# Masking the two large units of turned scores on TensorE instead of VectorE, with new orders on every engine and a setup that is split up among the first turns

## The reference

```
def _L0_attn_ref(X, ...):                     # one head, no mask
    A = softmax(Q K^T * scale);  return A V
def _L0_ffn_ref(x, w_gate, w_up, w_down):     # FP4 quantised inputs and weights
    h = silu(fp4_linear(x, w_gate)) * fp4_linear(x, w_up)
    return fp4_linear(h, w_down)
def _L1_attn_ref(inputs, qkv_kernel, qkv_bias):   # 16 heads of 8
    qk = jnp.einsum('bhse,bhte->bhst', q, k) * scale
    mask = jnp.triu(jnp.full((s, s), -jnp.inf, dtype=jnp.float32), k=1)
    attn = jax.nn.softmax(qk + mask, axis=-1)
def _L1_ffn_ref(x, gate_w, w1, w2, w3):       # 4 usable experts of 704, top 2 per token
    h = silu(x w1) * (x w3);  y = h w2;  out = sum of the two chosen
mod = (_silu(c) @ wmod)                       # 6 rows of 128 per sample and layer
x = x + ga * attn(layernorm(x) * (1 + ca) + sa)
x = x + gb * ffn(layernorm(x) * (1 + cb) + sb)   # this pair of lines twice
```

## Time and profile before

| | |
|---|---|
| profiled execution, span | 1905.3 us |
| the same execution's time | 1907.06 us |
| median of three runs | 1906.21 us |
| TensorE (PE) busy | 1699.7 us, 89% of the span |
| VectorE (DVE) busy | 1678.0 us, 88% |
| ScalarE (ACT) busy | 716.5 us, 38% |
| GpSimd (POOL) busy | 68.9 us, 4% |

### The profile page before, as it was taken

One profiled execution on the slowest core, in us unless ns is written; L12 is line 12 of the kernel. 1 busy time (PEld: TensorE's weight loads), 2 busy tenths in 40 slices (PEclk: granted clock), 3 DMA queues, 4 the chain that ended last, 5 costly groups with the idle time before them and its releaser, 6 DMA issues.

```text
span 1905.3 us, 37018 instructions
## 1 busy us (share of the span) xinstructions
PE 1699.7 (89%) x12297; PEld 1317.1 (69%) x12297; DVE 1678.0 (88%) x3791; ACT 716.5 (38%) x1447; POOL 68.9 (4%) x78
## 2 busy tenths in 40 slices
PE   2347799999999999999999999999999999999998
PEld 1234567776776767677686767777676777768787
DVE  5578799989899998989989998999989899997775
ACT  0122435262533426253432526243352525334332
POOL 0000000000000000000000000000000000000000
PEclk7686899999999999999999999999999999999999
DMA  4020302003030301203030110303021030303000
GB/s 142 25 76 28 109 5 89 28 20 98 5 107 10 104 14 27 86 15 97 10 105 13 50 63 18 99 5 106 12 63 51 18 99 6 100 10 91 12 13 8
DMA packets 130106, 97.25 MB, mean 51 GB/s; under 512 B 28000, under 2 KB 124512, under 8 KB 125824
## 3 DMA queue, kind: packets, MB, share of 16 engines
q1 hardware_dynamic: 121536, 91.74, 16.4%
q10 hardware_dynamic: 8448, 4.20, 0.7%
HBM read 56.48 MB, written 29.98 MB: 45 GB/s over the span
## 4 chain that ended last, share of the span: by engine, by line
PE 47%; DVE 37%; issue 9%; ACT 4%; SPq 1%; DVEq 1%; DMA 1%; POOL 0%; ACTq 0%; POOLq 0%
DVE mneg L1099 9%; PE y_ps L1476 9%; PE bank L1469 5%; PE bank L1471 5%; PE bank L1470 5%; DVE h L1196 4%; PE bank L1220 4%; DVE tt L1188 3%; PE bank L1436 3%; ACT arena L770 2%; DVE xh L967 2%; PE bank L1343 2%; DVE arena L1107 2%; PE bank L1373 2%; PE bank L1420 2%
## 5 line engine op out<-in xcount | busy, mean ns | idle before, releaser
L813 ACT ACTIVATE tt<-bank 128x512 f32<-128x512 f32 x352 | 212.4, 603 | 665.8 <-PE bank L1471 523.9
L1476 PEld LDWEIGHTS y_ps<-wd,h 128*128 128x128 f32 (+1 forms) x3072 | 379.1, 192 | 70.7 <-issue 19.1
L1476 PE MATMUL y_ps<-wd,h 128*128 128x128 f32 (+1 forms) x3072 | 415.4, 282 | 14.1 <-DVE h L1196 14.1
L1196 DVE TENSOR_TENSOR h<-tt,bank 128x512 f32<-128x512 f32 x352 | 236.0, 682 | 23.6 <-PE bank L1471 7.1
L1188 DVE SCALAR_TENSOR_TENSOR tt<-tt,bank 128x512 f32<-128x512 f32 x352 | 237.2, 682 | 21.4 <-ACT tt L813 14.7
L1099 DVE TENSOR_REDUCE mneg<-bank 128x2 f32<-128x512 f32 (+1 forms) x384 | 236.0, 680 | 3.9 <-issue 2.4
L770 ACT ACTIVATE arena<-bank 128x512 f32<-128x512 f32 x384 | 196.5, 612 | 34.8 <-PE bank L1417 20.7
L1469 PE MATMUL bank<-h_hi,wg_hi 128*128 128x512 f32 x352 | 164.2, 466 | 10.3 <-DVE h_lo L1163 3.8
L1469 PE MATMUL bank<-h_hi,wu_hi 128*128 128x512 f32 x352 | 163.1, 463 | 8.4 <-DVE mneg L1099 8.3
L1107 DVE TENSOR_TENSOR arena<-arena,keep_k 128x1024 f32<-128x1024 f32 (+1 forms) x96 | 149.0, 1577 | 20.4 <-ACT arena L770 18.8
L1471 PE MATMUL bank<-h_lo,wg_hi 128*128 128x512 f32 x352 | 140.5, 399 | 0.0
(11 more groups left out here) (183 smaller groups left out, 2647.0 us busy)
## 6 DMA issues: line engine op xcount, KB each, us to landing
q_stack<-q_rows SPq DMA_DIRECT2D x16, 1024.0 KB, 4.8
k_stack<-k_rows SPq DMA_DIRECT2D x16, 1024.0 KB, 8.0
q_rows<-qk_halves SPq DMA_DIRECT2D x48, 256.0 KB, 2.8
k_rows<-qk_halves SPq DMA_DIRECT2D x48, 256.0 KB, 2.9
rows<-mod_rows SPq DMA_DIRECT2D x48, 128.0 KB, 3.0
rows<-mod_rows SPq DMA_DIRECT2D x16, 384.0 KB, 3.5
x_in<-in_L_attn_X SPq DMA_DIRECT2D x16, 256.0 KB, 2.8
vals<-arena SPq DMA_DIRECT2D x128, 32.0 KB, 5.2
```

The source lines that it names most:

```text
L813: send(a(tt[:, ch % 2, :], ps.bank(f"eg{ch}")[:], ACT.Tanh, scale=0.5), tanh_ready)
L1196: frees(v.tensor_tensor(h32[:, ch % 3], tt[:, ch % 2, :], ps.bank(f"eu{ch}")[:], ALU.mult), f"eu{ch}")
L1476: ins = mm(y_ps[:, P * t:P * (t + 1)], h32[rows_, ch % 3, P * t:P * (t + 1)], wd[rows_, ch, :], start=first and t == 0, stop=last_ and t = ...
```

## The change

Four things are changed together.

1. *Masks.* `cover` is done for the four E units only (`covered` counts four instead of six). For L0 and L1, TensorE's `rows` first writes a mask to each of the four banks by `masked` with `mask_q` as the weights and `ident_b` as the moving side (a 128x512 bf16 matmul), and adds the sixteen products to it. `weigh` now waits for `covered` of its E unit and for ScalarE's last exponential of its L unit.
2. *Orders.* `USES` and the lists of SyncE, ScalarE, VectorE and TensorE are new. The point at which a turn begins has been moved as well: `maxima(5)`, `turn_max` and `stack_max` stood early in a turn with lead 1 and now stand at its end with lead 2.
3. *Setup loads.* The 31 loads of FP4 and expert weights are issued by ScalarE after its copy of the turned conditions. SyncE issues 15 small loads, the rows of ones and at once the first pair's `x_in`. The wait for the conditions counts four loads instead of all 15. The conditions lie in `mixed` instead of `x_in`, and the staging areas elsewhere in `arena`.
4. *Setup work.* The eight clamps become three wider ones. The two upper halves are copied by ScalarE. The rest is hung behind named steps of the first pair (`follow`): the quantisation of the first two weights behind `norm1`, the two lower halves behind `value0`, the third weight behind `quantise_x(2)` on VectorE; the turning of each weight on TensorE and its copy on ScalarE behind `scores0(1)`, `out0`, `probs0(1)` and `turn2`.

```diff
-SMALL = 15
+SMALL = 11
-USES = [(1, "SB30", "D", 6), (1, "SB31", "D", 5), ...
+USES = [(0, "eu6", "D", 3), (3, "T1", "A", 4), ...
 def sp_order(do):
-    do(1, "stack_v"), do(0, "load4"), do(1, "stack_max"), do(1, "load3"), do(1, "turn_att"), do(3, "load2"), do(4, "load1")
-    do(2, "store_q"), do(2, "store_k"), do(2, "stack")
+    do(1, "stack_v"), do(1, "load3"), do(0, "load4"), do(1, "turn_att"), do(3, "load2"), do(4, "load1"), do(2, "store_q")
+    do(2, "store_k"), do(2, "stack"), do(2, "stack_max")
...
-        covered = signal("covered", len(TURNED))
+        covered = signal("covered", len(EARLY))
...
-        def turns(eng, order, mine):
+        def turns(eng, order, mine, follow={}):
...
-                        mine[name](Turn(reg, plus + lead), *which)
+                        it = Turn(reg, plus + lead)
+                        mine[name](it, *which)
+                        if first_pair(it) and (name, *which) in follow:
+                            follow[(name, *which)]()
...
         def _(act):
-            act.wait_ge(s_ld, 16 * SMALL)
-            a(res[0:NB, 0:2, :], x_in[0:NB, 0:2, :], ACT.Tanh, scale=0.5).then_inc(s_act0, 1)
+            act.wait_ge(s_cond, 16 * 4)
+            a(res[0:NB, 0:2, :], mixed[0:NB, 0:2, :], ACT.Tanh, scale=0.5).then_inc(s_act0, 1)
             act.wait_ge(s_ct, 1)
             a(sct, y_ps[:, 0:2 * NB], ACT.Copy).then_inc(s_sct, 1)
...
+            act.dma_start(fp4_down, w_down).then_inc(s_fp4, 16)
...
+            act.wait_ge(s_w[0], 16 * 8)
+            a(wg_hi[:], stage[0], ACT.Copy).then_inc(s_split, 1)
+            act.wait_ge(s_w[1], 16 * 8)
+            a(wu_hi[:], stage[1], ACT.Copy).then_inc(s_split, 1)
+            act.wait_ge(s_ld, 16 * SMALL)
...
-            for j in (2, 5, 8, 11):
-                clamp(modt[:, j, :], modt[:, j, :], res[:, 0, 0:NB], res[:, 1, 0:NB])
+            gates = modt[:, 2:12:3, :]
+            clamp(gates, gates, *[res[:, n, 0:4 * NB].rearrange("p (j b) -> p j b", b=NB) for n in range(2)])
...
             def cover(it, u):
                 dve.wait_ge(*ps.is_freed(it, f"T{TURNED[u]}{GROUPS - 1}"))
-                n = S if TURNED[u] in EARLY else P
...
+            def lower_halves():
+                dve.wait_ge(s_split, 2)
+                v.tensor_tensor(wg_lo[:], stage[0], wg_hi[:].bitcast(F32), ALU.subtract).then_inc(s_ready, 1)
+                v.tensor_tensor(wu_lo[:], stage[1], wu_hi[:].bitcast(F32), ALU.subtract).then_inc(s_ready, 1)
...
-                            finish=finish))
+                            finish=finish), {("norm1",): fp4_halves, ("quantise_x", 2): fp4_third, ("value0",): lower_halves})
...
-            def masked(it, use, mask, cols_, n):
+            def masked(it, use, w, x, cols_, n):
                 free(it, use)
-                mm(cols_, ident_b[:], mask[:].unsqueeze(1).to_broadcast([P, n, P]), start=True, stop=False,
-                   skip_group_check=True)
+                mm(cols_, w[:], x[:].unsqueeze(1).to_broadcast([P, n, P]), start=True, stop=False, skip_group_check=True)
...
             def rows(it, u):
                 for g in range(GROUPS):
-                    free(it, use[g])
+                    if wide:
+                        free(it, use[g])
+                    else:
+                        masked(it, use[g], mask_q, ident_b, by_key(use[g], P), 4)
...
             def weigh(it, w):
-                after(it, covered, max(ue, ul) + 1)
+                after(it, covered, w + 1)
+                evacuated(it, f"T{TURNED[ul]}{GROUPS - 1}")
...
             def down(it, ch):
+                if first_pair(it):
+                    pe.wait_ge(s_wd, 16 * 2 * EXP)
```

258 lines of the change are left out of this document (135 added, 123 removed), and 46 rows, old and new, of the table USES.

## The result

| | before | after |
|---|---|---|
| median | 1905.7 us (8 runs, 1901.6 to 1909.7) | 1896.6 us (8 runs, 1891.7 to 1900.1) |
| ratio | | 0.995, 95% interval 0.9937 to 0.9963 |
| profiled execution, span | 1905.3 us | 1892.2 us |
| one turn of the loop | 109.8 us | 111.0 us |

Faster by 9 us; forecast were 33 (1873.0). 1896.6 lies just inside the forecast's own range (1850 to 1897), the turn of 111.0 outside its bounds (107.6 to 110.5). The setup gave more than the sum said, and then each turn took 1.2 us more where 0.8 less was forecast.

A forecast was written before the change was run, and what follows sets the result against it. Neither TensorE nor VectorE was taken as the bound alone; each sometimes waits for the other. 1907.06 - 26 (setup) - 10.4 (13 turns at 0.8) + 2.3 (last pair's masks) = 1873.0 us, own range 1850 to 1897.

The forecast's parts named there:

- The setup: Work ahead of the loop: loads, clamps and weight preparation rearranged so the first pair starts 26 us earlier, bounds 15 and 33.
- marks (27.4, near 66): Setup: first pair's transposes on TensorE start near 27.4 us instead of 61.09, its gate products near 66 instead of 91.98.
- Little from the setup: Rival, setup: ScalarE's weight loads land late or throughput bounds the fill; 10 us gained instead of 26, 1889 us; chance 0.13.
- The masks on TensorE: Loop: eight mask matmuls at 0.28 us each add 2.26 us per turn to TensorE; VectorE loses 4.6 us.
- Values late: Rival, loop: `vals` loads, now behind `stack_max`, delay `weigh(0)` by up to 0.5 us a turn; 1880 us; chance 0.05.
- How much of TensorE's idle time remains: Loop: of TensorE's 6.1 idle us per turn about 3.0 remain under the new orders; bounds 1.6 and 4.5.
- Turn: 106.0 + 3.0 = 109.0 us: Loop: TensorE's work plus remaining idle time per turn, 0.8 us less than before; bounds 107.6 to 110.5 us.
- 1.5 and 1.8: Loop, idle us left per turn: half the 3.0 of waits for maxima and products, and all 1.8 of smaller waits.
- The end: Drain after the loop: VectorE has slack and TensorE none, so the last pair's masks add 2.3 us.
- Masks whole: Rival, loop: the 6.1 idle us stay and masks add their full cost; 1912 to 1925 us; chance 0.17.
- VectorE was the bound: Rival, loop: TensorE had room, so the turn falls to 106.0 + 0.5 us and the kernel to 1840 us; chance 0.08.
- three signs of being wrong: TensorE's middle share staying at 94 to 95%, a turn below 107.5 us, or ScalarE's two copies ending after 35 us.

The follow-up runs named there:

- e_old_dve_s: Kernel after with the orders and bank table of before, all six covers on VectorE, plus 26 redundant instructions on VectorE in the setup: 1883.1 us.
- e_shift: Kernel after with 96 redundant wait instructions on TensorE in the setup, where it is idle, and nothing else: 1878.0 us.
- e_old_pe_s: Masks on TensorE with the orders of before and the new setup, padded by 169 instructions on TensorE and 30 on VectorE: 1875.0 us.
- e_mix_s: Kernel after with e_shift's waits, the loop boundary ahead of turn_max, and VectorE's logits and mix(2) ahead of quantise_x: 1883.4 us.
- e_old_dve: Kernel after with the orders and bank table of before, all six covers on VectorE and no new masks on TensorE: 1905.1 us.
- e_route_s: e_mix_s with VectorE's route moved behind times(21) and TensorE's down(18) put ahead of turn2: 1860.1 us.

## Why the prediction was wrong

**The setup: right.** Forecast 26 us; the first store came 30.5 us earlier (26.5 in e_old_dve_s, which has the old orders), and e_old_dve_s puts the worth of the whole part at 22.8 us. Its marks (27.4, near 66) were met within 0.4 us; ScalarE's copies were done at 32.9, 4 us later than thought, and nobody waited for them. "Little from the setup" was wrong.

**The masks on TensorE: right, the size a little high.** 0.24 us each instead of 0.28, 1.9 instead of 2.26 us per turn. The figure of the Trainium skill (TensorE: Matmul & The Clock Gate, Back-to-back issue gap) for an isolated matmul, 0.216, lies on the other side; its 131 ns for a stream of weight loads and matmuls is not borne out here. "Values late" was wrong: `vals` lands in 2.1 us, not 5.2.

**How much of TensorE's idle time remains: the step that failed.** The prediction wrote "Turn: 106.0 + 3.0 = 109.0 us" (its own terms for the 3.0, 1.5 and 1.8, add up to 3.3). It came to 111.0, of which TensorE is busy 106.5 and idle 4.5. The ten turns between the loop's marks cost 11.7 us where 8 were to be gained: 19.7 of the 23.6 us by which the forecast missed. All the waits of the earlier trace rows went, more than the half that I took, but two new ones came that the sum had no term for. The larger mistake is hole A: the loop's code moved in TensorE's instruction memory, because the setup part and the four turns ahead of the loop have other instruction counts (3281 records before, 3465 after). Taken away by e_shift it is worth 18.6 us, and then the turn is 109.24 us and the kernel 1878.0: 0.2 and 5 us from the forecast. That closeness is partly luck: hole B and VectorE's loss at the back edge are still in it, against lighter masks and more of the old waits gone, and an earlier first store against a longer end. "Nobody can read the new order's waits from a trace of the old one" was true of hole B. It was not true of hole A: the instruction count ahead of the loop and within it could have been counted from the changed kernel, though no trace of before said what a misplaced loop would cost.

**The end: too small.** 2.3 us forecast; from the loop's last mark to the last store it is 8.1 more, 8.3 in e_shift. e_old_dve_s has 339.9 us there and e_old_pe_s 334.8, so it is the new orders that cost this, not the masks. I charged only the last pair's masks and took the drain's order as neutral. These are single executions, 5 to 10 us apart.

**The rivals.** "Masks whole" fell: its mark, TensorE's share at 94 to 95%, was nearly met (96.0%), but for another reason, and in the old orders the masks made the turn shorter. "VectorE was the bound" was refuted as stated (the turn didn't reach 106.5), yet it is true of a stretch of some 25 us in each turn: hole B is VectorE's. The share over the whole turn (VectorE 89%, as forecast) hides a piece at 96% (23.9 of 25 us, e_mix_s). The rule of the Trainium skill (Perfetto Trace Analysis, Identifying the Most-Contended Engine), by the weight loads' share, points at VectorE as the bound, for which the prediction had 1840 us, and would have misled. None of the three signs of being wrong came (a share of 94 to 95%, a turn below 107.5, copies that end after 35 us): none of them looked for a turn that is longer than the forecast because new waits came.

**The sum with measured terms.** 1907.06 - 30.5 (first store) - 2.4 (to the loop) + 11.7 (ten turns) + 8.1 (end) = 1894.0, the profiled execution's 1893.94.

Open: the exact rule of hole A. My counts miss whatever code lies ahead of the kernel's own, so the places are off by a constant. If it is between 49 and 85, every kernel of the table falls into place: the loop stays where it touches seven blocks and is fetched anew where it touches eight. Why eight should not stay is open too, since by the skill's 2048 they would just fit; one block read ahead beyond the loop's end would explain that, and that then *nine* are fetched. This is argued from the table; no run shows the constant or the block ahead, and starts between 15 and 82 were not tried.

## What to carry to other kernels

Look at the DMA queues of kind "instruction" first when a loop grows or when code ahead of it changes: if packets run during the loop and TensorE's branch takes microseconds instead of 0.2, or VectorE's sequencer goes on later behind its branch than it did before the change, pad the code ahead of the loop and measure again before judging any other part of the change. A change that is several changes should be timed with its parts apart and with this confound removed; here it came to 19 to 33 us on TensorE and 22 on VectorE, as much as the setup's 23 and more than the masks' 8. And a wait on an engine whose list is full in that stretch isn't removed by reordering within the stretch: take work out of it, and check that the engine has idle time between two neighbouring waits before you count on one.

## What the runs showed of the hardware

- Where TensorE's loop of about 1700 instructions begins decides over 19 to 33 us of 1900: its back edge takes 0.2 us when nothing is fetched and 3.4 to 3.6 us when nine packets of 16 KB are, per turn.
- VectorE's loop (some 451 instructions) fetches five or six packets of 8 KB a turn on q14, in the kernel before too. With one of them between its branch and the next record of its sequencer, the sequencer goes on after 2.8 us (in single turns up to 3.1; loops that begin at 0, 4, 18, 21, 246, 249 and 255 modulo 256), with two after 3.4 to 3.5 us (252, e_old_dve; 247, e_mix_s). Which places give two I can't say. In the old orders the difference is worth 22 us (e_old_dve against e_old_dve_s).
- Queued long instructions cover VectorE's stop: with four reductions of 0.68 us queued 0.2 us were left idle in the kernel before, with nothing queued 2.3 us in e_shift.
- Behind waits of TensorE of 2.0 to 2.1 us in the kernel after, the granted clock was 0.52 and 0.55 over the next 3.4 and 3.6 us, but not always: behind the back edge it was at the lower level in six turns of ten, and behind the 1.7 to 1.8 us waits of e_shift in none of ten. In the kernels whose waits were at most 1.4 us (before, e_route_s) it was 1.00 over the middle, with two short spells at the lower level in the first and one in the second.
- A bf16 mask of 128x512 stands for 0.24 us from start to start when nothing is late around it, though its row says 388 ns.
